# A looped adjacency kernel written out straight, with block 0 loaded in whole chunks from two queues

## The chip, the cores and the metric

The kernel runs on one core of one Trainium2 chip. The metric is device time in microseconds (us), from three runs of the kernel before: 1064.25, 1066.31 and 1069.69, with a median of 1066.31.

## The reference

`x` is 8192x256, `adj` is 8192x8192 and `w` (L0_gnn_weight) is 256x256, all float32.

```
bw  = sign(w)                       # -1, 0, 1
ba  = maximum(sign(x), 0)           # 1 where x > 0
xw  = ba @ bw.T                     # 8192 x 256
agg = relu(adj @ xw)                # 8192 x 256, the large product
y   = x + agg
out = (y - mean(y)) / sqrt(var(y) + 1e-5)   # over each row of 256
```

`adj` alone is 268 MB, and it is read once.

## The kernel before

**Blocks, chunks, units.** The 8192 output rows are cut into 16 blocks of 512. A block needs all 8192 columns of its rows of `adj`, in 8 chunks of 1024 columns (2 MB each). A chunk lands in one of four slots of `raw` as four DMAs, one for each group of 32 partitions (a quadrant); in it each contiguous run is 256 elements, 1024 bytes. A chunk is 4 units, so a block is 32 units and the kernel 512.

**A unit.** `turn` (DVE, L450) transposes 32x32 squares into `turned` in SBUF, or for 10 of 32 units into `turned_v` in PSUM. `make_hi` (ACT, L326) rounds it to fp32r into one of six buffers of a ring. The rest, `lo`, is made by POOL (L299) for the 22 "P" units and by DVE (L456) for the 10 "V" units. `use_unit` (PE, L619) multiplies both parts with `xw`: 8 matmuls of 512 columns, or 8 pairs of weight load and matmul. The accumulators of a block are two banks of PSUM, and blocks alternate between two sets.

**The steps of xw.** `xw` (64 slices of 128x256) is made in 16 groups of four slices: `make_step` (DVE, L414) compares `x` with zero, `turn_step` (PE, L576) transposes it, a copy brings it to SBUF, `make_xw` (PE, L587) multiplies it with the signs of `w`, and `copy_xw` (ACT, L316) stores it over the `x` that it came from. Groups 0 to 9 are made ahead of the units (their middle copy is DVE's, L422, `copy_early_step`), in PSUM banks that they alternate between; groups 10 to 15 stand between units 0 to 24 (middle copy by ACT, L312, `copy_late_step`). Two units use one group.

**Loads of block 0.** All of block 0 is loaded from SP's queue: `x` in 32 DMAs of 256 KB (L205), in runs of 1024 bytes, and `adj` in 16 parts of two units (64 DMAs of 256 KB, L217), in runs of 512 bytes. ACT's queue takes part from block 1 on: SP starts the quadrants 0 and 1 of a chunk, ACT the quadrants 2 and 3 (`start_chunk`, L195), SP as soon as DVE has turned the last unit of the chunk four before, ACT in its own order after `make_hi` of that unit.

**The ending of a block** runs between the units of the next one: `make_relu` on ACT (L336) at its unit 5, `turn_back` on PE (L644, 8 transposes) after its unit 4, the sum with the rows of `x` and the statistics on DVE (L460 to L475), and `normalise` on ACT (L344). `make_relu` at unit 5 of ACT's order comes ahead of PE's unit 4, as ACT runs ahead.

**Loops.** Each engine's program is a function `pair(q)` of two blocks. Pair 0 is written out, and pairs 1 to 7 are a hardware loop, `Fori(1, PAIRS)`, on SP, POOL, DVE and PE. On ACT the loop has pairs 1 to 6, `Fori(1, PAIRS - 1)`, and pair 7 is written out behind it. In the loops the semaphore values and the source address of `adj` come from the loop's register. In time, the back edges of ACT's loop fall at the ends of blocks 3, 5, 7, 9 and 11; at the end of block 13 ACT leaves its loop, and the other engines take their last back edge.

```
            pair(0)
            with act.Fori(1, PAIRS - 1) as q:
                pair(q)
            pair(PAIRS - 1)
```

Of the kernel before, what the change touches and what calls it, by code (L numbers as in the profile page):

```python
# [3 lines left out]

P = 128
Q = 32
G = P // Q  # L20
BANK = 512


def build(nc, x, adj, w, out):
# [8 lines left out]
    PAIRS = NBLK // 2  # L33
# [5 lines left out]
    KB = KG // Q  # L39
    UK = 2  # L40
# [3 lines left out]
    UP = 2 * UB  # L44
# [4 lines left out]
    UPP = 2  # L49
    PARTS = UB // UPP  # L50
    XPARTS = 8
    XK = CH * KB // XPARTS
# [3 lines left out]
    EARLY = 10  # L56
    TURNED = UPP
    STEP_BUFS = 2

    def late(g, delay):  # L60


        return 3 * (g - EARLY) + delay

    STEP, TURN, COPY, XW, XW_COPY = 2, 2, 5, 4, 9
    assert all(late(g, XW_COPY) < g * UPG for g in range(EARLY, GROUPS))


# [3 lines left out]

    kinds = ["V" if n % UB * V_UNITS % UB < V_UNITS else "P" for n in range(UP)]
    per_pair = {k: kinds.count(k) for k in "PV"}

    assert per_pair["P"] % TP == 0 and "VV" not in "".join(kinds + kinds[:1])

    def known_met(value):

        return isinstance(value, int) and value <= 0  # L80

    def in_pair(n):

        return kinds[:n].count(kinds[n])

    def ordinal(q, n):

        return q * per_pair[kinds[n]] + in_pair(n)

    def ring_slot(n):  # L90

        s = n % RING
        return s, n - RING if n >= RING else max(m for m in range(UP) if m % RING == s) - UP


    adj_v = adj.rearrange("(q h t i) (c g k) -> q h c g i t k", h=2, t=NT, i=Q, c=CH, g=G)
    x_turn = x.rearrange("(c g b j) d -> c g j b d", c=CH, g=G, b=KB)
    x_rows = x.rearrange("(q h m p) d -> q h p m d", h=2, m=MT, p=P)
    out_rows = out.rearrange("(q h m p) d -> q h p m d", h=2, m=MT, p=P)
# [3 lines left out]
    with ctx:  # L103
# [37 lines left out]

        ps_xw = [ps[:, 2 * b * BANK:2 * (b + 1) * BANK].rearrange("p (k d) -> p k d", k=GK) for b in range(2)]
        xw_buf = [g % 2 if g < EARLY else 1 for g in range(GROUPS)]
# [4 lines left out]

        w_loaded = sem("w_loaded")
        x_loaded = [sem(f"x_loaded{i}") for i in range(XPARTS)]  # L150
        parts_loaded = [sem(f"parts_loaded{i}") for i in range(PARTS)]
# [11 lines left out]
        early_steps_copied = sem("early_steps_copied")  # L163
        late_steps_copied = sem("late_steps_copied")
# [21 lines left out]

        LOWER, UPPER = range(0, G // 2), range(G // 2, G)
        IN_TURNS = [g for both in zip(LOWER, UPPER) for g in both]  # L190

        def start_chunk(eng, q, h, c, quadrants):
            dst = raw[:, c % SLOTS, :].rearrange("p (t k) -> p t k", t=NT)
            for g in quadrants:
                eng.dma_start(dst[g * Q:(g + 1) * Q], adj_v[q, h, c, g]).then_inc(adj_loaded[c % SLOTS], 16)  # L195

        @block.sync
        def _(sp):
            sp.dma_start(w_sb, w_rows).then_inc(w_loaded, 16)

            def load_x(i):

                c, k = i * XK // KB, i * XK % KB
                for g in IN_TURNS:
                    sp.dma_start(x_sb[g * Q:(g + 1) * Q, i * XK:(i + 1) * XK],  # L205
                                 x_turn[c, g, :, k:k + XK]).then_inc(x_loaded[i], 16)

            def load_part(i):

                c, u = i * UPP // UPC, i * UPP % UPC  # L210
                k0, k1 = u * UK * Q, (u + UPP) * UK * Q
                dst = raw[:, c % SLOTS, :].rearrange("p (t k) -> p t k", t=NT)
                if c >= SLOTS:

                    sp.wait_ge(units_turned, (c - SLOTS) * UPC + u + UPP)
                for g in IN_TURNS:
                    sp.dma_start(dst[g * Q:(g + 1) * Q, :, k0:k1],  # L217
                                 adj_v[0, 0, c, g, :, :, k0:k1]).then_inc(parts_loaded[i], 16)

            def load_chunk(q, h, c):  # L220
                n = (q * 2 + h) * CH + c

                sp.wait_ge(units_turned, (n - SLOTS + 1) * UPC)
                start_chunk(sp, q, h, c, LOWER)

            def block_before(q, h):
                return (q, 0) if h else (q - 1, 1)

            def store_rows(q, h):
                sp.wait_ge(blocks_done, q * 2 + h + 1)  # L230
                sp.dma_start(out_rows[q, h], rows[:]).then_inc(rows_stored, 16)

            def load_rows(q, h):
                b = q * 2 + h
                if known_met(b):
# [5 lines left out]
                sp.dma_start(rows[:], x_rows[q, h]).then_inc(rows_loaded, 16)  # L241

            def load_block_0():

                early = EARLY * GK // XK
                for i in range(early - 1):
                    load_x(i)
                for i in range(PARTS):
                    for j in range(early, XPARTS):
                        if late(j * XK // GK, STEP) == i * UPP:  # L250
                            load_x(j)
                    load_part(i)
                    if i == 0:
                        load_x(early - 1)

            def load_block(q, h):
                for c in range(CH):
                    load_chunk(q, h, c)

                    if c == 2 and not known_met(q * 2 + h - 1):  # L260
                        store_rows(*block_before(*block_before(q, h)))
                    if c == 3:
                        load_rows(*block_before(q, h))

            load_block_0()
            load_block(0, 1)
            with sp.Fori(1, PAIRS) as q:
                for h in range(2):
                    load_block(q, h)
            store_rows(PAIRS - 1, 0)  # L270
            load_rows(PAIRS - 1, 1)
            for b, ms in PIECES:
                if b == NBLK - 1:
                    sp.wait_ge(blocks_done, NBLK)
                else:
                    sp.wait_ge(last_piece_done, 1)
                sp.dma_start(out_rows[PAIRS - 1, 1, :, ms[0]:ms[-1] + 1],
                             rows[:, ms[0]:ms[-1] + 1]).then_inc(rows_stored, 16)
            sp.wait_ge(rows_stored, (NBLK - 1 + len(PIECES)) * 16)

        @block.gpsimd
        def _(pool):
# [8 lines left out]
            def pair(q):  # L291
                for n in range(UP):
                    if kinds[n] != "P":
                        continue
                    t = in_pair(n) % TP
                    s, _ = ring_slot(n)

                    pool.wait_ge(his_made, q * UP + n + 1)  # L298
                    pool.tensor_tensor(lo[:, s], turned[:, t], hi[:, s].bitcast(f32),  # L299
                                       ALU.subtract).then_inc(p_los_made, 1)  # L300

            pair(0)
            with pool.Fori(1, PAIRS) as q:
                pair(q)

        @block.scalar
        def _(act):
            def copy_late_step(n):
                act.wait_ge(steps_turned, n + 1)

                act.wait_ge(xw_made, n - 1)
                act.activation(step_xT[:, n % 2], ps_xT[n % 2], ACT.Copy).then_inc(late_steps_copied, 1)  # L312

            def copy_xw(n):
                act.wait_ge(xw_made, n + 1)
                act.activation(xw[:, n * GK:(n + 1) * GK], ps_xw[xw_buf[n]], ACT.Copy).then_inc(xw_copied, 1)  # L316

            def make_hi(q, n):
                s, prev = ring_slot(n)
                act.wait_ge(units_turned, q * UP + n + 1)  # L320
                if not known_met(q * UP + prev + 1):

                    act.wait_ge(units_used, q * UP + prev + 1)
                t = in_pair(n)
                src = turned[:, t % TP] if kinds[n] == "P" else turned_v
                act.activation(hi[:, s], src, ACT.Copy).then_inc(his_made, 1)  # L326

            def make_relu(q, h):
                b = q * 2 + h
                act.wait_ge(first_halves, b + 1)  # L330
                if not known_met(b):
                    act.wait_ge(relus_turned, b * MT)
                for a in range(DH):
                    if a == 1:
                        act.wait_ge(units_used, (b + 1) * UB)
                    act.activation(relu[:, a], acc[h][a], ACT.Relu).then_inc(relus_made, 1)  # L336

            def make_std(b, ms):
                act.wait_ge(mvs_made, b + 1)
                act.activation(std[:, ms], mv[:, ms, 1], ACT.Sqrt, bias=eps[:]).then_inc(stds_made, 1)  # L340

            def normalise(b, m, last):
                act.wait_ge(shifts_made, b + 1)
# [5 lines left out]
            def ending(q, h, u):  # L349

                if u == RING - 1:
                    make_relu(q, h)
# [341 lines left out]
```

## Time and profile before

| | us |
|---|---|
| Median of the runs (1064.25 to 1069.69) | 1066.31 |
| Span of the profiled execution, first to last instruction | 1064.2 |
| PE busy with matmuls | 993.5 |
| DVE busy | 858.2 |
| POOL busy | 840.3 |
| ACT busy | 605.2 |
| Data moved | 294.36 MB, 277 GB/s over the span |
| Mean granted TensorE clock | 0.976 |

The span is one profiled execution and not one of the three runs; the device time of that execution is not given by itself, so the span is the profiled execution's own time here. An average over the span hides the stages: block 0, the blocks after it, and the last few microseconds each have another limit.

### The profile page before, as it was taken

To read this page: it belongs to the slowest core of one execution; us is meant where nothing else is said; L and a number is where in the kernel's file an instruction comes from. 1 tells how busy PE (TensorE), PEld (TensorE's weight loads), DVE (VectorE), ACT (ScalarE), POOL (GpSimd) and SP (SyncE) were. 2 spreads that over 40 slices of the span, in tenths; PEclk is the share of its full clock that TensorE was granted. 3 is DMA by queue.
4 is the path that set the end of the run, shared out by engine and by line. 5 is a ranking of instruction groups with operands and counts; after the bars stand their busy time and mean duration, and the time that the engine had idled before them with its cause. 6 is when DMAs were issued, how large, how long until landed. Compare 5 with 4: busy or idle time off the path is not lost.

```text
span 1064.2 us, 15065 instructions
## 1 busy us (share of the span) xinstructions
PE 993.5 (93%) x4484; PEld 812.8 (76%) x4484; DVE 858.2 (81%) x881; ACT 605.2 (57%) x647; POOL 840.3 (79%) x361
## 2 busy tenths in 40 slices
PE   5578699999998999899998999899998999999996
PEld 4356578888877888788886888778886888888885
DVE  4656489898959989598886989599895989799893
ACT  3345366666546656466565665466564665566562
POOL 0346489899868988599896998599885998889893
PEclk9889899999999999999999999989999999999999
DMA  9999999999998999899998999999998999999961
GB/s 216 226 223 224 228 286 320 302 332 317 308 315 241 292 324 282 250 295 311 299 297 250 300 313 294 290 236 289 327 284 253 300 306 299 300 290 297 309 198 39
DMA packets 313166, 294.36 MB, mean 277 GB/s; under 512 B 9760, under 2 KB 313120, under 8 KB 313120
## 3 DMA queue, kind: packets, MB, share of 16 engines
q1 hardware_dynamic: 186400, 168.06, 62.3%
q10 hardware_dynamic: 126720, 125.84, 42.3%
q14 instruction: 36, 0.29, 0.1%
q8 instruction: 10, 0.16, 0.1%
HBM read 285.47 MB, written 8.39 MB: 276 GB/s over the span
## 4 chain that ended last, share of the span: by engine, by line
PE 44%; POOL 26%; issue 12%; SPq 9%; DMA 4%; DVE 3%; ACT 1%; POOLq 0%; ACTq 0%
PE ps L619 44%; POOL lo L299 26%; SPq L217 7%; DMA raw<-in_adj_dram 4%; SPq L205 2%; DVE turned L450 1%; DVE lo L456 1%; PE ps L644 1%; DVE ps L450 0%; ACT hi L326 0%; DVE relu L414 0%; DVE stats L464 0%; POOLq L298 0%; SPq L195 0%; ACT rows L344 0%
## 5 line engine op out<-in xcount | busy, mean ns | idle before, releaser
L299 POOL TENSOR_TENSOR lo<-turned,hi 128x1024 fp32r<-128x1024 f32 x352 | 839.2, 2413 | 207.1 <-ACT hi L326 203.9
L619 PE MATMUL ps<-hi,xw 128*128 128x512 f32 x2048 | 810.0, 396 | 31.8 <-DVE lo L456 27.1
L619 PE MATMUL ps<-lo,xw 128*128 128x512 f32 x2048 | 804.8, 393 | 0.0
L326 ACT ACTIVATE hi<-turned 128x1024 fp32r<-128x1024 f32 x352 | 373.4, 1061 | 281.4 <-DVE turned L450 161.7
L619 PEld LDWEIGHTS ps<-hi,xw 128*128 128x128 f32 x2048 | 389.6, 190 | 120.0 <-DVE lo L456 24.9
L619 PEld LDWEIGHTS ps<-lo,xw 128*128 128x128 f32 x2048 | 389.4, 190 | 80.4
L450 DVE STREAM_TRANSPOSE turned<-raw 128x1024 f32<-128x1024 f32 x352 | 426.1, 1218 | 22.3 <-DMA raw<-in_adj_dram 22.3
L456 DVE TENSOR_TENSOR lo<-ps,hi 128x1024 fp32r<-128x1024 f32 x160 | 194.8, 1217 | 128.1 <-ACT hi L326 127.5
L326 ACT ACTIVATE hi<-ps 128x1024 fp32r<-128x1024 f32 x160 | 164.1, 1025 | 134.4 <-issue 58.9
L450 DVE STREAM_TRANSPOSE ps<-raw 128x1024 f32<-128x1024 f32 x160 | 195.1, 1219 | 18.6 <-DMA raw<-in_adj_dram 18.6
L344 ACT ACTIVATE rows<-rows,shift,rstd 128x256 f32<-128x256 f32 x62 | 36.4, 588 | 0.0
L587 PE MATMUL ps<-sign_wT,rows 128*128 128x256 bf16 x128 | 21.3, 325 | 13.1 <-ACT xw L316 11.5
L460 DVE TENSOR_TENSOR rows<-ps,rows 128x1024 f32<-128x1024 f32 (+1 forms) x17 | 19.4, 1139 | 13.5 <-PE ps L644 12.2
L587 PEld LDWEIGHTS ps<-sign_wT,rows 128*128 128x128 bf16 x128 | 13.7, 115 | 19.2 <-issue 13.3
L414 DVE TENSOR_SCALAR relu<-x_sb 128x1024 bf16<-128x1024 f32 x16 | 16.6, 1046 | 12.4 <-DMA x_sb<-in_x_dram 12.4
L316 ACT ACTIVATE xw<-ps 128x1024 fp32r<-128x1024 f32 x16 | 16.3, 1020 | 12.5 <-PE ps L587 12.5
L576 PE MATMUL ps<-ident_b,relu 128*128 128x128 bf16 x128 | 12.0, 254 | 11.9 <-DVE relu L414 11.9
L336 ACT ACTIVATE relu<-ps 128x512 f32<-128x512 f32 x32 | 17.2, 586 | 9.2 <-PE ps L619 9.2
L464 DVE BATCH_NORM_STATS2 stats<-rows 128x6 f32<-128x256 f32 x64 | 22.3, 409 | 0.1
L576 PEld LDWEIGHTS ps<-ident_b,relu 128*128 128x128 bf16 x128 | 9.7, 116 | 15.0 <-DVE relu L414 13.2
L644 PE MATMUL ps<-ident,relu 128*128 128x128 f32 x128 | 16.8, 273 | 0.2 <-ACT relu L336 0.2
L644 PEld LDWEIGHTS ps<-ident,relu 128*128 128x128 f32 x128 | 14.8, 140 | 2.7 <-ACT relu L336 0.4
(23 smaller groups left out, 47.8 us busy)
## 6 DMA issues: line engine op xcount, KB each, us to landing
raw<-in_adj_dram ACTq DMA_DIRECT2D x240, 512.0 KB, 10.4
raw<-in_adj_dram SPq DMA_DIRECT2D x240, 512.0 KB, 9.0
raw<-in_adj_dram SPq DMA_DIRECT2D x64, 256.0 KB, 7.4
x_sb<-in_x_dram SPq DMA_DIRECT2D x32, 256.0 KB, 8.1
rows<-in_x_dram SPq DMA_DIRECT2D x16, 512.0 KB, 8.8
out_dram<-rows SPq DMA_DIRECT2D x15, 512.0 KB, 13.7
out_dram<-rows SPq DMA_DIRECT2D x2, 256.0 KB, 2.3
rows<-in_L_gnn_weight_dram SPq DMA_DIRECT2D x1, 256.0 KB, 3.7
```

The lines of the kernel that those rows point to most:

```text
L205: sp.dma_start(x_sb[g * Q:(g + 1) * Q, i * XK:(i + 1) * XK], x_turn[c, g, :, k:k + XK]).then_inc(x_loaded[i], 16)
L217: sp.dma_start(dst[g * Q:(g + 1) * Q, :, k0:k1], adj_v[0, 0, c, g, :, :, k0:k1]).then_inc(parts_loaded[i], 16)
L299: pool.tensor_tensor(lo[:, s], turned[:, t], hi[:, s].bitcast(f32), ALU.subtract).then_inc(p_los_made, 1)
L326: act.activation(hi[:, s], src, ACT.Copy).then_inc(his_made, 1)
L344: done = act.activation(rows[:, m], rows[:, m], ACT.Identity, bias=shift[:, m:m + 1], scale=rstd[:, m:m + 1])
L450: dve.transpose(dst.rearrange("p (k t j) -> p k t j", k=UK, j=Q), src).then_inc(units_turned, 1)
L456: dve.tensor_tensor(lo[:, s], turned_v[:, :], hi[:, s].bitcast(f32), ALU.subtract).then_inc(v_los_made, 1)
L464: dve.bn_stats(stats[:, m], rows[:, m]).then_inc(stats_made, 1)
L576: last = pe.transpose(ps_xT[n % 2][:, k, i], step_x[:, n % STEP_BUFS, k, i * P:(i + 1) * P], ident_b[:])
L587: last = pe.matmul(ps_xw[xw_buf[n]][:, k], step_xT[:, n % 2, k, i], sign_wT[:, i], start=(i == 0), stop=(i == DH - 1))
L619: return pe.matmul(acc[h][a], xw[:, step, a * P:(a + 1) * P], part[:, s, k * MB:(k + 1) * MB], start=(step == 0 and part is hi), stop=(ste ...
L644: last = pe.transpose(back[:, m, a * P:(a + 1) * P], relu[:, a, m * P:(m + 1) * P], ident[:])
```

## The change

The program becomes straight on every engine: no loops, and all semaphore values and addresses are constants. The order of the units, the engine that takes each, the ring and the endings are the same. In block 0:

- `adj` comes from both queues, SP the quadrants 0 and 1, ACT the quadrants 2 and 3. Chunk 0 comes in two halves (runs of 512 bytes, 8 DMAs of 256 KB), chunks 1 to 7 whole (runs of 1024 bytes, 28 DMAs of 512 KB).
- `x` comes from both queues too, in 9 pieces (36 DMAs): two of four slices for chunk 0, then one of eight slices for each chunk, issued just ahead of the chunk.
- ACT issues `x` and chunks 0 and 1 ahead of its first copy, `x` and chunk 2 ahead of `copy_xw(0)`, `x` and chunk 3 after `make_hi(1)`, and from then on a chunk (with its `x` in block 0) after each fourth unit.
- Only groups 0 and 1 of the steps start ahead of the units; the others stand between the units of block 0, one group for each two units. ACT makes all the middle copies, and one pair of PSUM banks holds the product.

```diff
+    X_PIECES = [(0, GK), (GK, GK)] + [(c * KB, KB) for c in range(1, CH)]
...
         @block.sync
+            for i in range(2):
+                start_x(sp, i, LOWER)
+                start_half(sp, i, LOWER)
...
+            for c in range(1, CH):
+                start_x(sp, c + 1, LOWER)
+                load_chunk(c)
+            for b in range(1, NBLK):
                 for c in range(CH):
-                    load_chunk(q, h, c)
+                    load_chunk(b * CH + c)
...
         @block.scalar
-            act.wait_ge(idents_made, 3)
-            for g in range(EARLY - XK // GK):
-                copy_xw(g)
-            for n in range(TURNED):
-                make_hi(0, n)
-            for g in range(EARLY - XK // GK, EARLY):
-                copy_xw(g)
-            pair(0)
-            with act.Fori(1, PAIRS - 1) as q:
-                pair(q)
-
-            pair(PAIRS - 1)
...
+            for i in range(2):
+                start_x(act, i, UPPER)
+                start_half(act, i, UPPER)
+            start_x(act, 2, UPPER)
+            start_chunk(act, 1, UPPER)
+            copy_step(0)
+            start_x(act, 3, UPPER)
+            start_chunk(act, 2, UPPER)
+            copy_xw(0)
+            for n in range(UNITS):
+                make_hi(n)
+                if n == 0:
+                    copy_step(1)
+                if n == 1:
+                    start_x(act, 4, UPPER)
+                    start_chunk(act, 3, UPPER)
+                ch = n // UPC + SLOTS
+                if n % UPC == UPC - 1 and ch < NCHUNK:
+                    if ch < CH:
+                        start_x(act, ch + 1, UPPER)
+                    start_chunk(act, ch, UPPER)
+                if n < UB:
+                    g = n // UPG + 1
+                    if n % UPG and 2 <= g < GROUPS:
+                        copy_step(g)
+                    if n % UPG and g - 1 >= 1:
+                        copy_xw(g - 1)
+                else:
+                    ending(n // UB - 1, n % UB)
...
         @block.vector
-            dve.wait_ge(signs_turned, 1)
-            dve.tensor_copy(sign_wT[:], ps_wT).then_inc(signs_copied, 1)
...
             make_step(0)
-            for g in range(1, EARLY):
...
-            pair(0)
-            with dve.Fori(1, PAIRS) as q:
-                pair(q)
+            dve.wait_ge(signs_turned, 1)
+            dve.tensor_copy(sign_wT[:], ps_wT).then_inc(signs_copied, 1)
+            for n in range(UNITS):
+                turn(n)
+                if n == 0:
+                    make_step(1)
+                if n and kinds[n - 1] == "V":
+                    make_lo(n - 1)
+                c = n // UPC + 1
+                if n % UPC == UPC - 1 and c < CH:
+                    for g in range(c * KB // GK, (c + 1) * KB // GK):
+                        make_step(g)
+                if n >= UB:
+                    ending(n // UB - 1, n % UB)
...
         @block.tensor
-            pair(0)
-            with pe.Fori(1, PAIRS) as q:
-                pair(q)
-            turn_back(PAIRS - 1, 1)
+            turn_step(0)
+            pe.wait_ge(signs_copied, 1)
+            make_xw(0)
+            turn_step(1)
+            for n in range(UNITS):
+                use_unit(n)
+                if n < UB and n % UPG == 0:
+                    g = n // UPG
+                    if g + 1 < GROUPS:
+                        make_xw(g + 1)
+                    if g + 2 < GROUPS:
+                        turn_step(g + 2)
+                if n >= UB and n % UB == BACK_AT:
+                    turn_back(n // UB - 1)
+            turn_back(NBLK - 1)
```

`UNITS` is 512, `UB` 32 (units of a block), `UPC` 4 (of a chunk), `UPG` 2 (of a group), `SLOTS` 4. `make_xw(n)` waits for `copy_step(n)` and `copy_xw(n - 1)`, `use_unit` of an even unit 2g of block 0 for `copy_xw(g)`, and `copy_step(n)` for `make_xw(n - 2)`.

## Rows read from the trace of the kernel before

**Rows 1.** The page: busy time of each engine, and GB/s in 40 slices.
```profile
PE 993.5 (93%) x4484; PEld 812.8 (76%) x4484; DVE 858.2 (81%) x881; ACT 605.2 (57%) x647; POOL 840.3 (79%) x361
...
GB/s 216 226 223 224 228 286 320 302 332 317 308 315 241 292 324 282 250 295 311 299 297 250 300 313 294 290 236 289 327 284 253 300 306 299 300 290 297 309 198 39
```

**Rows 2.** Timeline of PE, the transposes of the block endings (start us, us, engine, line).
```profile
150.42 1.04 PE L644 MATMUL ps<-ident,relu 128*128 128x128 f32 x8
...
209.37 1.03 PE L644 MATMUL ps<-ident,relu 128*128 128x128 f32 x8
...
268.29 1.04 PE L644 MATMUL ps<-ident,relu 128*128 128x128 f32 x8
...
333.27 1.03 PE L644 MATMUL ps<-ident,relu 128*128 128x128 f32 x8
...
828.03 1.03 PE L644 MATMUL ps<-ident,relu 128*128 128x128 f32 x8
...
1004.83 1.04 PE L644 MATMUL ps<-ident,relu 128*128 128x128 f32 x8
```

**Rows 3.** Timeline, ACT and PE behind the end of block 3.
```profile
320.00 1.02 ACT L326 ACTIVATE hi<-ps 128x1024 fp32r<-128x1024 f32 x1 [11.39 <-issue]
...
322.34 0.50 PE L619 MATMUL ps<-hi,xw 128*128 128x512 f32 x1 [4.01 <-DVE lo L456]
```

**Rows 4.** Timeline of ACT behind the end of block 13, where it leaves its loop.
```profile
937.09 1.07 ACT L326 ACTIVATE hi<-turned 128x1024 fp32r<-128x1024 f32 x1 [0.75 <-PE ps L619]
937.11 0.87 ACTq L195 DMA_DIRECT2D raw<-in_adj_dram  x2
938.08 1.03 ACT L326 ACTIVATE hi<-ps 128x1024 fp32r<-128x1024 f32 x1
```

**Rows 5.** Windows: busy us (x instructions) by engine, PEclk, DMA share, GB/s.
```profile
0.00:4.00 4.00, 0.00 (x0) 0.00 (x0) 0.00 (x0) 0.00 (x0) 1.12 (x9) 1.00 0.54 128
...
4.00:16.00 12.00, 6.07 (x41) 4.52 (x42) 6.04 (x10) 2.31 (x2) 0.00 (x0) 1.00 1.12 236
60.00:90.00 30.00, 20.36 (x111) 15.79 (x111) 21.70 (x18) 16.18 (x17) 14.39 (x7) 0.89 1.21 224
...
172.00:192.00 20.00, 20.00 (x90) 16.57 (x89) 18.89 (x18) 14.35 (x17) 19.53 (x10) 1.00 1.10 347
936.00:948.00 12.00, 12.00 (x59) 10.02 (x58) 11.33 (x11) 9.19 (x11) 12.00 (x6) 1.00 1.12 235
```

**Rows 6.** The page, queue of ACT: packets, MB, share.
```profile
q10 hardware_dynamic: 126720, 125.84, 42.3%
```

**Rows 7.** Timeline: DMAs issued by SP and ACT in block 0 (start, duration of issue).
```profile
1.23 11.16 SPq L205 DMA_DIRECT2D x_sb<-in_x_dram  x16
...
26.51 18.86 SPq L217 DMA_DIRECT2D raw<-in_adj_dram  x12
...
92.00 4.81 ACTq L195 DMA_DIRECT2D raw<-in_adj_dram  x1
...
97.45 1.03 ACT L326 ACTIVATE hi<-ps 128x1024 fp32r<-128x1024 f32 x1 [3.67 <-issue]
```

**Rows 8.** Timeline of PE in block 0: a product of xw, a unit, transposes, a unit.
```profile
85.42 1.03 PE L587 MATMUL ps<-sign_wT,rows 128*128 128x256 bf16 x8 [3.09 <-ACT xw L316]
86.21 0.47 PE L619 MATMUL ps<-hi,xw 128*128 128x512 f32 x1
...
88.14 0.62 PE L576 MATMUL ps<-ident_b,relu 128*128 128x128 bf16 x8
88.57 0.47 PE L619 MATMUL ps<-hi,xw 128*128 128x512 f32 x1
...
90.50 0.40 PE L619 MATMUL ps<-hi,xw 128*128 128x512 f32 x1
```

**Rows 9.** Timeline of ACT in block 0.
```profile
98.37 1.02 ACT L312 ACTIVATE rows<-ps 128x1024 bf16<-128x1024 bf16 x1
99.28 1.06 ACT L326 ACTIVATE hi<-turned 128x1024 fp32r<-128x1024 f32 x1
100.22 1.02 ACT L316 ACTIVATE xw<-ps 128x1024 fp32r<-128x1024 f32 x1
```

**Rows 10.** The page, costliest groups: busy, mean ns, idle before.
```profile
L299 POOL TENSOR_TENSOR lo<-turned,hi 128x1024 fp32r<-128x1024 f32 x352 | 839.2, 2413 | 207.1 <-ACT hi L326 203.9
...
L450 DVE STREAM_TRANSPOSE turned<-raw 128x1024 f32<-128x1024 f32 x352 | 426.1, 1218 | 22.3 <-DMA raw<-in_adj_dram 22.3
```

More of the change, by code:

```diff
@@ L55, in build, with ordinal, piece_of_group @@
     UPG = GK // UK
-    EARLY = 10
-    TURNED = UPP
     STEP_BUFS = 2
[L60 to L66, printed above, removed]
+    BACK_AT = 4
     PIECES = [(NBLK - 1, range(0, MT // 2)), (NBLK, range(MT // 2, MT))]
[L73 to L96, printed above, removed]
+    kinds = ["V" if n * V_UNITS % UB < V_UNITS else "P" for n in range(UB)] * NBLK
+    before = {k: [0] * (UNITS + 1) for k in "PV"}
+    for n, kind in enumerate(kinds):
+        for k in "PV":
+            before[k][n + 1] = before[k][n] + (k == kind)
+    assert "VV" not in "".join(kinds) and kinds[-1] == "P"
+    def ordinal(n):
+        return before[kinds[n]][n]
+    X_PIECES = [(0, GK), (GK, GK)] + [(c * KB, KB) for c in range(1, CH)]
+    def piece_of_group(g):
+        return g if g < KB // GK else g * GK // KB + 1
+    adj_v = adj.rearrange("(b t i) (c g k) -> b c g i t k", t=NT, i=Q, c=CH, g=G)
     x_turn = x.rearrange("(c g b j) d -> c g j b d", c=CH, g=G, b=KB)
-    x_rows = x.rearrange("(q h m p) d -> q h p m d", h=2, m=MT, p=P)
-    out_rows = out.rearrange("(q h m p) d -> q h p m d", h=2, m=MT, p=P)
+    x_rows = x.rearrange("(b m p) d -> b p m d", m=MT, p=P)
+    out_rows = out.rearrange("(b m p) d -> b p m d", m=MT, p=P)
     w_rows = w.rearrange("(a p) i -> p a i", p=P)
@@ L139, in build @@
         turned_v = ps[:, 4 * BANK:6 * BANK]
-        ps_xw = [ps[:, 2 * b * BANK:2 * (b + 1) * BANK].rearrange("p (k d) -> p k d", k=GK) for b in range(2)]
-        xw_buf = [g % 2 if g < EARLY else 1 for g in range(GROUPS)]
+        ps_xw = ps[:, 2 * BANK:4 * BANK].rearrange("p (k d) -> p k d", k=GK)
         ps_xT = [ps[:, b * BANK:(b + 1) * BANK].bitcast(bf16).rearrange("p (k a n) -> p k a n", k=GK, a=DH)
@@ L199, in _, with load_chunk, store_rows, load_rows @@
             sp.dma_start(w_sb, w_rows).then_inc(w_loaded, 16)
[L201 to L235, printed above, removed]
+            for i in range(2):
+                start_x(sp, i, LOWER)
+                start_half(sp, i, LOWER)
+            def load_chunk(ch):
+                if ch >= SLOTS:
+                    sp.wait_ge(units_turned, (ch - SLOTS + 1) * UPC)
+                start_chunk(sp, ch, LOWER)
+            def store_rows(b):
+                sp.wait_ge(blocks_done, b + 1)
+                sp.dma_start(out_rows[b], rows[:]).then_inc(rows_stored, 16)
+            def load_rows(b):
+                if b == 0:
                     sp.wait_ge(xw_made, GROUPS)
@@ L240, in load_rows @@
                     sp.wait_ge(rows_stored, b * 16)
[L241 to L256, printed above, removed]
+                sp.dma_start(rows[:], x_rows[b]).then_inc(rows_loaded, 16)
+            for c in range(1, CH):
+                start_x(sp, c + 1, LOWER)
+                load_chunk(c)
+            for b in range(1, NBLK):
                 for c in range(CH):
-                    load_chunk(q, h, c)
-                    if c == 2 and not known_met(q * 2 + h - 1):
-                        store_rows(*block_before(*block_before(q, h)))
+                    load_chunk(b * CH + c)
+                    if c == 2 and b >= 2:
+                        store_rows(b - 2)
                     if c == 3:
[L263 to L271, printed above, removed]
+                        load_rows(b - 1)
+            store_rows(NBLK - 2)
+            load_rows(NBLK - 1)
             for b, ms in PIECES:
@@ L289, in _ @@
                                    pattern=[[-1, P]], channel_multiplier=1).then_inc(idents_made, 1)
[L291 to L299, printed above, removed]
+            for n in range(UNITS):
+                if kinds[n] == "P":
+                    pool.wait_ge(his_made, n + 1)
+                    pool.tensor_tensor(lo[:, n % RING], turned[:, ordinal(n) % TP], hi[:, n % RING].bitcast(f32),
@@ L314, in copy_xw @@
             def copy_xw(n):
                 act.wait_ge(xw_made, n + 1)
[L316 to L326, printed above, removed]
@@ L328, in make_relu, with make_hi @@
-            def make_relu(q, h):
-                b = q * 2 + h
+                act.activation(xw[:, n * GK:(n + 1) * GK], ps_xw, ACT.Copy).then_inc(xw_copied, 1)
+            def make_hi(n):
+                act.wait_ge(units_turned, n + 1)
+                if n >= RING:
+                    act.wait_ge(units_used, n - RING + 1)
+                src = turned[:, ordinal(n) % TP] if kinds[n] == "P" else turned_v
+                act.activation(hi[:, n % RING], src, ACT.Copy).then_inc(his_made, 1)
@@ L330, in make_relu @@
+            def make_relu(b):
                 act.wait_ge(first_halves, b + 1)
-                if not known_met(b):
+                if b:
                     act.wait_ge(relus_turned, b * MT)
@@ L366, in pair @@
-            def pair(q):
-                for n in range(UP):
-                    if not (known_met(q) and n < TURNED):
-                        make_hi(q, n)
-                        load_chunk_after(q, n)
-                    for g in range(EARLY, GROUPS):
-                        if known_met(q) and n == late(g, COPY):
-                            copy_late_step(g)
-                        if known_met(q) and n == late(g, XW_COPY):
-                            copy_xw(g)
-                    if n < UB and not known_met(q):
-                        ending(q - 1, 1, n)
-                    if n >= UB:
-                        ending(q, 0, n - UB)
@@ L397, in _ @@
+            make_relu(NBLK - 1)
+            for n, ms in PIECES:
+                make_std(n, slice(ms[0], ms[-1] + 1))
+            n, ms = PIECES[0]
             for m in ms:
-                normalise(b, m, m == ms[-1])
+                normalise(n, m, m == ms[-1])
         @block.vector
@@ L580, in make_xw @@
             def make_xw(n):
-                wait_step_copied(n)
-                if n >= 2:
-                    pe.wait_ge(xw_copied, max(m for m in range(n) if xw_buf[m] == xw_buf[n]) + 1)
+                pe.wait_ge(steps_copied, n + 1)
+                if n >= 1:
+                    pe.wait_ge(xw_copied, n)
                 for k in range(GK):
                     for i in range(DH):
-                        last = pe.matmul(ps_xw[xw_buf[n]][:, k], step_xT[:, n % 2, k, i], sign_wT[:, i],
+                        last = pe.matmul(ps_xw[:, k], step_xT[:, n % 2, k, i], sign_wT[:, i],
@@ L647, in turn_back @@
                             last.then_inc(relus_turned, 1)
-            BACK_AT = 4
-            def pair(q):
-                for n in range(UP):
-                    for g in range(EARLY, GROUPS):
-                        if known_met(q) and n == late(g, TURN):
-                            turn_step(g)
-                        if known_met(q) and n == late(g, XW):
-                            make_xw(g)
-                    use_unit(q, n)
-                    if n == BACK_AT and not known_met(q):
-                        turn_back(q - 1, 1)
-                    if n == UB + BACK_AT:
-                        turn_back(q, 0)
-            pair(0)
-            with pe.Fori(1, PAIRS) as q:
-                pair(q)
-            turn_back(PAIRS - 1, 1)
+            turn_step(0)
+            pe.wait_ge(signs_copied, 1)
+            make_xw(0)
+            turn_step(1)
+            for n in range(UNITS):
+                use_unit(n)
[8 more added lines that the diff above has]
+            turn_back(NBLK - 1)
 _INS = ['x', 'adj', 'L0_gnn_weight']
```

221 lines of the change are left out of this document (84 added, 137 removed).

## The prediction

> **What bounds the kernel now.** I read the page first, then the stages. PE is busy 93% of the span and the others less; the slices of GB/s [rows 1] fall into a start of some 140 us at about 225 GB/s and a rest near 300, with a dip at 241, 250, 250, 236 and so on every 120 us or so. So there are three stages: block 0, the blocks after it, and their interruptions.
>
> The transposes of the endings stand at one place of every block and serve as a clock [rows 2]. Where nothing interferes two of them are 58.95 or 58.92 us apart, and the last three blocks take (1004.83 - 828.03) / 3 = 58.93 each. That is PE itself: 256 matmuls at 0.227 plus 0.87 for the transposes. POOL needs 22 x 2.41 = 53.1 of them, DVE has 32 turns at 1.22 and 10 los [rows 10]. From 150.42 to 1004.83 are 14 blocks, 14 x 58.93 = 825.0, but 854.4 passed: 29.4 us are lost. They are lost behind blocks 3, 5, 7, 9 and 11, and nowhere else (268.29 to 333.27 is 64.98, 6.05 too much; the other four cost 5.5 to 6.5). There ACT stands 11.39 us with no releaser, only "issue", and PE waits 4.01 for the lo behind it [rows 3], then runs its first matmuls at the lower clock. Those are the five places where ACT's loop takes its back edge. Behind block 13 all the other engines take theirs, ACT does not, and ACT goes on without a gap [rows 4]. So ACT's back edge costs, and theirs does not.
>
> The span is thus: ending of block 0 at T1 = 150.42, 825.0 for 14 blocks, 29.4 lost, and 59.4 from the last ending's place to the end (1064.2 - 1004.83).
>
> In block 0 PE is busy about two thirds of the time (20.4 of 30 us) while the DMA share is full [rows 5]: data bound it. One queue moves 236 GB/s in runs of 1024 bytes (the first x) and 224 with runs mostly of 512, so the length of the runs alone is worth 5%. With both queues filled it is 347 [rows 5]. Behind block 13 it falls to 235 again, in runs of 1024 bytes, for 12 us.
>
> **The change, part by part.**
>
> *Straight program.* No back edge remains: minus 29.4 us. What must hold is that straight code of this length is fetched in time; ACT's pairs 0 and 7 are straight now, and pair 7 shows no gap at its start [rows 4]. In the loops the waits on register values vanish too, which I cost at nothing: PE's 58.93 hides them. The 14 blocks now follow one another without a rest for the DMA queues. A block needs 16.8 MB of adj and 1 MB of rows in 58.93 us, 302 GB/s, against 347 when both queues are full [rows 5]; so 825.0 stays.
>
> *Bytes of block 0.* x is 8.39 MB, adj 16.78, w 0.26: 25.4 MB. At 347 GB/s, with 1.8 us of start (4 us at 128 GB/s are 2.2 us at 236 [rows 5]), the last chunk would have landed at 75; halves of chunk 0 are 512-byte runs, and I put everything up to them at 300. Between 236 and 347 this landing is at 110 to 75. Before, T1 less five units puts the end of block 0 at 141.
>
> *PE in block 0.* Two units share a group of xw. From the rows: product 0.79 (85.42 to 86.21), a unit 1.93 (86.21 to 88.14), transposes 0.43, a unit 1.93 [rows 8]: 5.08 us for two units, 81 us for the block. PE's order makes a chain: even unit 1.93, product 0.79, transposes 0.62 until their end, then on ACT the middle copy and copy_xw, 0.92 and 1.02 [rows 9], and only then the next even unit: 5.4 with 0.1 for the handing over. So 5.4 per group, 10.8 per chunk; a chunk and its x are 3.15 MB, 9.1 us at 347. Fully loaded, PE's chain is slower than the data. ACT has 2 x 1.05 + 1.94 = 4.0 in those 5.4, POOL at most 4.8: hidden.
>
> *ACT's own DMA issues.* This is the part that costs. A queue takes only so much: by 12.39 us SP had issued 16 x DMAs, 4,096 runs [rows 7], while 0.51 MB + 8.4 us x 236 GB/s - 0.26 = 2.2 MB had moved: 1,900 runs were outstanding, and SP needed 0.70 us for each issue. By 45.37 it had issued 14,336 runs and some 12,700 had moved, 1,650 outstanding. I take 1,750 to 1,800 runs as the limit (packets of ACT's queue are one for a run of 1024 bytes, [rows 6]). Now ACT issues the same amounts, and its copies stand behind. Its half of x and chunks 0 and 1 is 4,096 runs, x and chunk 2 and each later one 1,536 more. So copy_step(0) has to wait until 2,300 runs of ACT's have moved, copy_xw(0) for 3,830, make_hi(2) for 5,370, and copy_step(2), behind unit 3 and chunk 4, for 6,900. Those are for both halves 3.1, 6.0, 9.2 and 12.3 MB, or 12, 21, 30 and 39 us (3.4 MB at 300, the rest at 347). PE starts unit 0 at about 23, and unit 2 waits for copy_xw(1), which ACT does behind copy_step(2): 40.7. Chunk 5 is behind unit 7, at 47.5, where its room is there at 47.8: from then on ACT no longer waits. Nothing of this is seen on ACT now but one issue of 4.81 us, behind which a hi stood 3.67 us late [rows 7].
>
> From unit 2 on: 15 groups, 14 x 5.4 + 3.9 = 79.5, plus 2 for the lower clock after PE's idle 13 us, gives 122 for the end of block 0. Five units of block 1, 9.3, give T1 = 131.5 against 150.4: minus 18.9.
>
> **Sum.** 131.5 + 825.0 + 59.4 = 1015.9 against the profiled 1064.2, so minus 48.3. The median of the runs is 2.1 above that span: 1066.3 - 48.3 = 1018.0.
>
> **A rule that speaks against it.** The Trainium skill, in "DMA: Bandwidth & Descriptors", section "Issuing engines are not separate DMA queues", says that DMAs started by several engines run on the same 16 DMA engines and that the only saving is the issuing time. The trace disagrees for this shape: 235 to 236 with one queue, 347 with two [rows 5]. By the rule block 0 would stay at 236; that is rival 2.
>
> **Rivals.**
>
> 1. *ACT's issues don't hold it.* For: in the steady blocks two DMAs of ACT take 0.87 [rows 4]. Against: there its queue is never full, and SP's was [rows 7]. Then unit 4 starts as chunk 1 has landed (22.5) and been turned, at 27.5; 14 groups later, less 1.5 for the last, it is 101.6, T1 = 111, and the time 997.
>
> 2. *The two queues don't add up in block 0*, where x and adj are mixed: 236 GB/s. A chunk with x takes 13.4 us, ACT waits for 12.3 MB until 54, and again ahead of chunk 8: 8,704 + 3 x 1,536 + 1,024 - 1,800 runs, 107 us, with 12 units left after unit 19: 32 us more. T1 = 148, and only the 29.4 and 2 are won: 1035.
>
> 3. *The gaps stay.* ACT's 11.39 has no releaser in the profile; that the back edge makes it is read from where it falls. If it comes back as often in straight code, 29.4 stay: 1047.
>
> 4. *Slower: straight code stalls.* A fetch that costs ACT 11 us and PE 5.9 would come at each stretch of code not seen before, and now all of it is new. The mechanism needs more than 48.3 / 5.9 = 8 such gaps beyond the five of now to lose: two in each of 14 blocks, 28 in all, are 23 more than now, plus 136 - 18.9: 1183; one for each block, 14, gives 1066 + 53 - 18.9 = 1100. Against it: no such gap in the straight pairs.
>
> Beside rivals 3 and 4 stands a rule: the Trainium skill, in "Runtime: NRT & Kernel Launch", section "Instruction fetch mechanics", has straight code fetched ahead and a taken branch outside the fetched pages wait for its target. By it both rivals fall; the trace agrees at ACT's five back edges and shows no cost at the other engines'.
>
> **How the numbers follow.** Forecast: 0.50. Its own range is 1008 to 1028: with 355 GB/s and a limit of 2,050 runs copy_step(2) comes 2 us earlier, with 310 and 1,500 it comes 5 later, and 15 groups at 5.1 to 5.6 are 4.5 less or 3 more. Rival 1: 0.18. Rival 2: 0.14. Rival 3: 0.07. Rival 4: 0.06. Nothing gained, for a reason that I don't see: 0.05. The range takes in rivals 1 and 2 and ends just beyond them, 995 to 1036; rivals 3 and 4 and the last case are left out, 0.18. A measurement of this kernel tells about 0.5% from no change, 5.3 us. Faster by more: forecast, rivals 1, 2 and 3, and a little of the last, 0.90. Same 0.03, slower 0.07.
>
> **What would show it.** Right: transposes of the endings 58.93 apart from first to last, no idle "issue" on ACT behind block 1; first of them near 131; ACT's DMA issues of several us each before unit 4, and "issue" as what ended ACT's idle time there; PE idle for over 10 us ahead of unit 2; 330 GB/s or more from 15 to 60 us. Wrong: issues of 0.4 us on ACT and a first ending at 111 (rival 1); a rate of 236 in block 0 (rival 2); ACT idle for 11 us at regular places (rivals 3 and 4), or waits for raw in the blocks after 0, which would tell that the DMA needed its rests.

## The result, and the profile after

The changed kernel takes 1021.75 us (median; 1067.2 before, in four runs each): 0.958 of the time before, with a 95% interval of 0.955 to 0.960. The forecast was 1018.0. One of the four executions took 1054.4 and is left out of the ratio; it has no trace, and e4's profiled one, 1055.6, shows what such an execution can look like. The profiled execution has a span of 1019.9 and a device time of 1021.75.

| | before | after |
|---|---|---|
| Span of the profiled execution | 1064.2 | 1019.9 |
| First ending's transposes (T1) | 150.4 | 134.9 |
| From there to the last ending but one (14 blocks) | 854.4 | 825.1 |
| From there to the end | 59.4 | 59.9 |

Timeline of PE in the kernel after, the transposes of the endings (start us, us, engine, line). They answer to [rows 2].

```profile
134.87 1.04 PE L500 MATMUL ps<-ident,relu 128*128 128x128 f32 x8
...
193.82 1.03 PE L500 MATMUL ps<-ident,relu 128*128 128x128 f32 x8
...
959.98 1.04 PE L500 MATMUL ps<-ident,relu 128*128 128x128 f32 x8
```

Two endings are 58.95 us apart, and (959.98 - 134.87) / 14 is 58.94: no block loses anything now. 29.3 us of the gain are there, and 15.5 in block 0. The page's rows for [rows 1]:

```profile
PE 977.7 (96%) x4484; PEld 802.9 (79%) x4484; DVE 846.3 (83%) x871; ACT 614.0 (60%) x657; POOL 841.7 (83%) x361
...
GB/s 284 346 314 230 180 294 310 307 283 315 297 305 306 317 297 291 327 286 302 299 318 292 299 294 315 297 304 323 274 317 291 317 291 311 321 277 320 288 180 41
```

The dips to 240 and 250 every 120 us are gone, and the start has 346 where it had 225. The fourth and fifth slices, 230 and 180, are low for another reason: by then the data are ahead of PE, and SP waits until DVE has turned the units of a chunk and freed its slot. The windows of block 0 (busy us by engine, PEclk, DMA share, GB/s), for [rows 5]:

```profile
4.00:16.00 12.00, 3.65 (x24) 2.65 (x25) 5.25 (x7) 2.31 (x2) 0.00 (x0) 1.00 1.17 283
16.00:40.00 24.00, 8.23 (x40) 5.87 (x37) 7.72 (x7) 7.85 (x9) 7.02 (x3) 0.89 1.10 346
...
60.00:90.00 30.00, 27.50 (x164) 20.45 (x162) 21.29 (x20) 19.55 (x21) 16.63 (x8) 1.00 1.08 280
```

PE is busy for 8.2 of the 24 us from 16 to 40, while the queues move data at 346 GB/s. What it waits for stands in ACT's timeline (bracket: idle before, and what ended it):

```profile
4.87 3.40 ACTq L169 DMA_DIRECT2D x_sb<-in_x_dram  x2
8.30 3.17 ACTq L155 DMA_DIRECT2D raw<-in_adj_dram  x2
...
12.80 1.02 ACT L240 ACTIVATE rows<-ps 128x1024 bf16<-128x1024 bf16 x1
...
15.22 4.49 ACTq L155 DMA_DIRECT2D raw<-in_adj_dram  x2
19.75 1.02 ACT L244 ACTIVATE xw<-ps 128x1024 fp32r<-128x1024 f32 x1 [5.93 <-issue]
...
24.73 4.41 ACTq L155 DMA_DIRECT2D raw<-in_adj_dram  x2
29.19 1.06 ACT L251 ACTIVATE hi<-turned 128x1024 fp32r<-128x1024 f32 x1 [5.64 <-DVE ps L352]
...
33.43 4.42 ACTq L155 DMA_DIRECT2D raw<-in_adj_dram  x2
37.95 1.02 ACT L240 ACTIVATE rows<-ps 128x1024 bf16<-128x1024 bf16 x1 [6.76 <-issue]
```

Issues of 0.3 to 0.5 us elsewhere take 2.2 each here. The 5.64 us ahead of `make_hi(2)` are put down to DVE, but the copy starts at 29.19, just as the issue of 24.73 ends (29.14): there too the issue ended last. ACT's first copy starts at 12.8, copy_xw(0) at 19.75, make_hi(2) at 29.19 and copy_step(2) at 37.95 (forecast: 12, 21, 30, 39). PE's unit 2 follows:

```profile
39.95 0.79 PE L475 MATMUL ps<-hi,xw 128*128 128x512 f32 x1 [9.36 <-ACT xw L244]
```

### The profile page after: what moved, and what is told of

Its sections match the earlier page's. It is cut to its first block, busy times and chain, and to the rows that moved or that the text cites. A ratio compares the mean times of both kernels' runs of the same rounds, so it can differ in the third digit from the quotient of the medians.

```text
span 1019.9 us, 12240 instructions
## 1 busy us (share of the span) xinstructions
PE 977.7 (96%) x4484; PEld 802.9 (79%) x4484; DVE 846.3 (83%) x871; ACT 614.0 (60%) x657; POOL 841.7 (83%) x361
## 4 chain that ended last, share of the span: by engine, by line
PE 92%; ACTq 3%; ACT 2%; issue 2%; DVE 1%; DVEq 0%
PE ps L475 89%; ACTq L155 2%; PE ps L500 1%; ACT xw L244 1%; ACTq L169 1%; PE ps L460 1%; PE ps L450 1%; DVE relu L330 1%; ACT hi L251 0%; ACTq L162 0%; DVE stats L364 0%; ACT L240 0%; DVE rows L360 0%; ACT rows L240 0%; ACT relu L260 0%
## 5 line engine op out<-in xcount | busy, mean ns | idle before, releaser
L475 PEld LDWEIGHTS ps<-hi,xw 128*128 128x128 f32 x2048 | 385.6, 188 | 102.7 <-ACT xw L244 17.1
L240 ACT ACTIVATE rows<-ps 128x1024 bf16<-128x1024 bf16 x16 | 16.4, 1025 | 34.8 <-PE ps L450 28.0
L460 PE MATMUL ps<-sign_wT,rows 128*128 128x256 bf16 x128 | 18.8, 295 | 6.1 <-ACT rows L240 6.1
L500 PEld LDWEIGHTS ps<-ident,relu 128*128 128x128 f32 x128 | 14.8, 140 | 2.7 <-ACT relu L260 0.4
## 6 DMA issues: line engine op xcount, KB each, us to landing
rows<-in_x_dram SPq DMA_DIRECT2D x16, 512.0 KB, 11.3
```

The costliest lines, as they stand in the source:

```text
L460: last = pe.matmul(ps_xw[:, k], step_xT[:, n % 2, k, i], sign_wT[:, i], start=(i == 0), stop=(i == DH - 1))
L475: return pe.matmul(acc[b % 2][a], xw[:, step, a * P:(a + 1) * P], part[:, n % RING, k * MB:(k + 1) * MB], start=(step == 0 and part is hi) ...
L500: last = pe.transpose(back[:, m, a * P:(a + 1) * P], relu[:, a, m * P:(m + 1) * P], ident[:])
```

## The experiments

Those on the kernel before are e1 and e2; all others are edits of the changed kernel. Each was timed against the kernel before, whose medians were 1064.97 to 1067.41 in these sessions.

**e1: ACT's loop alone written out.**

```diff
-            with act.Fori(1, PAIRS - 1) as q:
+            for q in range(1, PAIRS - 1):
                 pair(q)
```

> The kernel before with ACT's loop alone written out; block 0 and the loops of SP, POOL, DVE and PE stay. Theory (only ACT's back edge costs, 5.9 us of PE each): the five gaps go, 29.4 us less, about 1037.5, and the endings' transposes stand 58.93 apart from block 1 on. Rival (the gap comes with the amount of ACT's code, not with the back edge): ACT still stands 11 us at five or more places, 1067 or more. Rival (the other engines' back edges cost PE too and hide behind ACT's): between 1040 and 1067.

Measured: 1035.94, a ratio of 0.972 (0.968 to 0.975). The endings' transposes in its timeline:

```profile
149.25 1.03 PE L644 MATMUL ps<-ident,relu 128*128 128x128 f32 x8
...
974.36 1.03 PE L644 MATMUL ps<-ident,relu 128*128 128x128 f32 x8
```

14 blocks take 825.1, or 58.94 each, with the loops of the four other engines in place. So ACT's loop alone, with its back edges, made the 29.4. The time is 1.6 below the 1037.5 expected.

**e2: the loops of SP, POOL, DVE and PE written out, ACT's left.** The edit is that of e1 on the other four engines.

> The kernel before with the loops of SP, POOL, DVE and PE written out, ACT's loop left. Theory: no change, 1067, ACT's five gaps of 11 us and PE's of 4 us remain behind blocks 3, 5, 7, 9 and 11. Rival (others' back edges cost as well): 5 us or more faster. Rival (long straight code of PE costs fetches): slower, by 5.9 us for each.

Measured: 1067.62 (median of ten) beside 1065.77 before, which is 1.002 of it. The ratio of 0.996 (0.990 to 1.001) takes in only the three lowest of the ten. Either way there is no change. ACT's gap stands where it stood:

```profile
320.03 1.02 ACT L326 ACTIVATE hi<-ps 128x1024 fp32r<-128x1024 f32 x1 [11.33 <-issue]
```

One of the ten executions took 1050.5; it has no trace, and why is open. Together e1 and e2 settle rivals 3 and 4 of the prediction: straight code has no gaps of its own, neither on ACT nor on PE.

**e3: all loads of block 0 on SP's queue, in the changed kernel's pieces.**

```diff
-                start_x(sp, i, LOWER)
-                start_half(sp, i, LOWER)
+                start_x(sp, i, IN_TURNS)
+                start_half(sp, i, IN_TURNS)
...
-                start_x(sp, c + 1, LOWER)
+                start_x(sp, c + 1, IN_TURNS)
```

`IN_TURNS` are the quadrants 0, 2, 1, 3, so that the one queue changes between the halves of the partitions. `load_chunk` does the same for block 0, and ACT starts none of its DMAs there.

> The changed kernel with all loads of block 0 on SP's queue, in the same pieces (runs of 1024 bytes but for chunk 0), and none on ACT. Theory (the rate comes from the two queues, the length of the runs gives 5%): 236 GB/s in block 0, the last chunk lands near 110 us, ACT's issues no longer hold it, first ending near 132, time about 1019. Rival (the rate of 347 comes from whole chunks in long runs, whichever queue): 347 GB/s from SP alone, no stalls of ACT, first ending near 111, time about 998.

Measured: 1036.23, ratio 0.972 (0.969 to 0.976): 14.5 slower than the changed kernel. Its windows, and the first ending:

```profile
4.00:16.00 12.00, 4.52 (x28) 2.91 (x28) 6.10 (x8) 4.24 (x5) 0.00 (x0) 1.00 1.15 235
16.00:40.00 24.00, 16.87 (x71) 12.69 (x72) 14.01 (x11) 10.62 (x11) 11.65 (x5) 0.88 1.13 225
...
60.00:90.00 30.00, 23.97 (x132) 17.46 (x131) 17.18 (x15) 16.03 (x18) 15.09 (x6) 0.94 1.13 225
```

```profile
149.48 1.03 PE L488 MATMUL ps<-ident,relu 128*128 128x128 f32 x8
```

The rate is 225 with runs of 1024 bytes, as the 224 with runs of mostly 512 before [rows 5]. So whole chunks bring nothing by themselves: the first ending is at 149.5, where it was before, and block 0's gain needs ACT's queue beside SP's.

The expected 132 for that ending was 17 too early. 25.4 MB at 225 instead of 236 is 5 later. The rest stands in DVE's timeline, at the first unit of chunk 7:

```profile
126.76 1.25 DVE L340 STREAM_TRANSPOSE turned<-raw 128x1024 f32<-128x1024 f32 x1 [3.76 <-DMA raw<-in_adj_dram]
```

By then 28.5 MB had moved (counted by queue in the trace), 2.6 of them on ACT's queue and all for block 1: they went ahead of chunk 7, which needs only block 0's 25.4.

The same trace says two things more. The first is that a second queue alone does not bring the rate. From 96 to 112 us both queues move data, SP 1.9 MB (all quadrants) and ACT 1.8 MB (quadrants 2 and 3), and the sum is that of one queue. In the kernel before it is the same from 98 to 118, 228 GB/s.

```profile
96.00:112.00 16.00, 10.41 (x63) 7.66 (x62) 1.37 (x2) 5.47 (x6) 2.37 (x1) 0.91 1.12 235
```

346 came only where SP's queue writes the quadrants 0 and 1 and ACT's the quadrants 2 and 3. Whether the separate halves make it is not tested: no run has two queues over the same halves throughout. The DMA share does not tell the two cases apart, 1.12 at 235 and 1.10 at 346.

The second is that an issue can be slow with nothing ahead of it on its own queue. This is the first DMA that ACT starts in e3, while SP's queue is full; its first bytes move at 93.4.

```profile
80.98 7.00 ACTq L156 DMA_DIRECT2D raw<-in_adj_dram  x1
```

**e4: ACT issues the same DMAs later among its copies.**

```diff
+            later = {1: 2, 3: 3, 5: 4, 7: 5, 11: 6, 15: 7}
...
+                    if n in later:
+                        start_x(act, later[n] + 1, UPPER)
+                        start_chunk(act, later[n], UPPER)
```

Chunk 1 goes behind `copy_step(0)`, and the old places of the issues are gone.

> The changed kernel; ACT issues the same DMAs of block 0 later among its copies: chunk 1 behind the first middle copy, chunk 2 behind unit 1, chunks 3, 4 and 5 behind the copies of units 3, 5 and 7. Theory (units 0 to 3 wait because ACT stands in issues of chunks that they don't need): unit 2 starts near 26 us instead of 39.9, first ending near 122 instead of 134.9, time about 1009. Rival (block 0 is bound by its data or by PE's chain, whatever ACT does early): less than 2 us gained, 1020 to 1022. Rival (ACT's queue runs empty and the rate falls to 236 at times): first ending above 135, slower than 1022.

Measured: 1015.99, ratio 0.954 (0.950 to 0.957), 5.8 less where 13 were expected. Of its five executions the profiled one took 1055.6, late chunks from 480 us on; block 0 is read from it, where it is not disturbed. The first ending is at 128.74. In ACT's timeline units 2 and 3 come at 19.75 instead of 29.19 and 30.16, behind a first stall of 3.3, but three longer ones follow, ahead of units 4, 6 and 8:

```profile
29.19 1.02 ACT L251 ACTIVATE hi<-ps 128x1024 fp32r<-128x1024 f32 x1 [5.61 <-issue]
...
37.99 1.06 ACT L251 ACTIVATE hi<-turned 128x1024 fp32r<-128x1024 f32 x1 [5.01 <-issue]
...
48.23 2.00 ACT L251 ACTIVATE hi<-turned 128x1024 fp32r<-128x1024 f32 x2 [6.44 <-issue]
```

A chunk behind each two units is more than the queue drains: the stall moves with the issue. That ACT's issues bind is shown; how much is to be had was not, so far.

**e5: copy_xw ahead of the next middle copy.**

```diff
+                    if n % UPG and g - 1 >= 1:
+                        copy_xw(g - 1)
                     if n % UPG and 2 <= g < GROUPS:
                         copy_step(g)
-                    if n % UPG and g - 1 >= 1:
-                        copy_xw(g - 1)
```

> The changed kernel; in block 0 ACT makes copy_xw ahead of the middle copy of the next group. Theory (the chain unit, product, transposes, two copies sets 5.48 us for two units): a copy leaves the chain and PE's own 5.08 is left, 0.4 us x 13 groups = 5 us less, about 1016.5. Rival (PE's own work or the waits on lo set the period): no change.

Measured: 1014.95, ratio 0.951 (0.950 to 0.953), first ending at 128.98: 5.9 less. The median is 6.8 less, where 5 were expected. The chain through ACT's two copies was real.

**e6: DVE makes the steps ahead of the lo.** In the kernel after, ACT's middle copies follow one another by 5.47 to 5.51 us but for two places of 7.5, at unit 11 (56.67 to 64.16) and unit 27. DVE's timeline there:

```profile
59.56 1.23 DVE L356 TENSOR_TENSOR lo<-ps,hi 128x1024 fp32r<-128x1024 f32 x1 [5.41 <-ACT hi L251]
60.70 3.35 DVE L330 TENSOR_SCALAR relu<-x_sb 128x1024 bf16<-128x1024 f32 x2
```

and PE's:

```profile
63.51 0.62 PE L450 MATMUL ps<-ident_b,relu 128*128 128x128 bf16 x8 [1.84 <-DVE relu L330]
```

Units 10 and 26 are V units and next to last in their chunk, so DVE waits with their lo for ACT and only then makes the steps that PE's transposes need. The edit moves the loop over `make_step` ahead of `make_lo`.

> The changed kernel; DVE makes the two steps at the end of a chunk ahead of the lo of the unit before. Theory (at units 11 and 27 that lo waits for ACT's hi, and PE's transposes wait for the step behind it, 2 us each): the two periods of 7.5 us become 5.5, 4 us less, about 1017.7. Rival (the steps are late for their x or for the step buffers): no change.

Measured: 1018.28, ratio 0.954 (0.953 to 0.956), first ending at 130.52, 4.35 earlier. Its profiled execution, 1022.5, lost 5 us again, in the blocks after 0, to late chunks, most of them between 480 and 760.

**e7: e4, e5 and e6 together.**

> The changed kernel with ACT's issues later, copy_xw first and the steps ahead of the lo, all three. Theory: they add up, 13 + 5 + 4 = 22 us less, near 1000, limited by the landing of the chunks: chunk 7 lands at 77 and PE needs 10.2 us for a chunk, so the data does not bind. Rival (with PE faster the data of block 0 binds): the gain stops at about 15 us, 1007.

Measured: 1009.46, ratio 0.947 (0.944 to 0.950), first ending at 120.07, in six executions from 1007.1 to 1016.9. 14.8 in block 0, close to what the three gave singly (6.1 + 5.9 + 4.35 = 16.4). The 22 expected are missed because e4's part was put at 13. The time is near the rival's 1007, but e10 below shows that the data of block 0 were not the limit here. Every group of two units in the middle of block 0 now takes PE's own time (transposes behind products, 5.06 apart):

```profile
59.98 0.61 PE L445 MATMUL ps<-ident_b,relu 128*128 128x128 bf16 x8
...
65.03 0.61 PE L445 MATMUL ps<-ident_b,relu 128*128 128x128 bf16 x8
...
70.09 0.61 PE L445 MATMUL ps<-ident_b,relu 128*128 128x128 bf16 x8
```

**e8: ACT's issues of block 0 spread out.**

```diff
-            later = {1: 2, 3: 3, 5: 4, 7: 5, 11: 6, 15: 7}
+            later = {1: 2, 5: 3, 9: 4, 12: 5, 15: 6, 18: 7}
```

> As e7, with ACT's issues of chunks 3 to 7 of block 0 spread to stand behind units 5, 9, 12, 15 and 18 (in e7: 3, 5, 7, 11 and 15, where ACT still stood in four issues, 21 us in all, up to 48 us). Theory (the queue takes some 2,000 runs, 1.3 chunks with x; a chunk for each four units never fills it): no gaps of ACT after 20 us, unit 2 near 24, 15 groups at 5.06, first ending near 109 instead of 120.1, time near 997. Rival (the queue runs empty or the chunks land late): waits for raw in block 0, first ending at 115 or more. The blocks after 0 may still lose some us to late chunks, as in e7.

Measured: 1007.54, ratio 0.945 (0.943 to 0.946), in seven executions from 1006.8 to 1026.3; first ending at 121.19. The expected 109 was missed, and block 0 is no shorter than in e7 (120.07). From 20 to 47 us no copy of ACT waited for an issue, but chunks 5 to 8 stand close together, and there ACT had four waits of 2.3, 2.5, 4.6 and 4.7, each of which ended as an issue ended (seen in e9's trace, which has the same schedule; the last of them):

```profile
69.24 5.70 ACTq L155 DMA_DIRECT2D raw<-in_adj_dram  x2
74.99 1.02 ACT L241 ACTIVATE xw<-ps 128x1024 fp32r<-128x1024 f32 x1 [4.71 <-issue]
```

**e9: e8, with the rows stored from ACT's queue.** In SP's program the stores of blocks 0 to 14 go, and ACT has:

```diff
+                if u == 27:
+                    act.wait_ge(blocks_done, b + 1)
+                    act.dma_start(out_rows[b], rows[:]).then_inc(rows_stored, 16)
```

> As e8, with the store of each block's rows issued by ACT at unit 27 in place of SP in the next block. Now SP's queue moves 9.4 MB a block and ACT's 8.4; this makes it 8.9 and 8.9. Theory (in straight blocks of 58.93 us SP's queue is the one that falls behind, 302 GB/s wanted of 347): the late chunks of e7's blocks 13 and 14 go, the runs lie closer together (within 3 us) and the median is 2 to 5 us below e8. Rival (the lag is of the memory, not of a queue): scatter and median as e8.

Measured: 1006.38, ratio 0.943 (0.942 to 0.945), five executions from 1005.9 to 1007.7. The longest waits of e8 from 120 us on have these two rows:

```profile
DVE turned L348 <- DMA raw<-in_adj_dram: 18.8, 11, 4.1
...
DVE rows L356 <- DMA rows<-in_x_dram: 15.6, 8, 2.3
```

e9's have no wait for a DMA at all. The medians are 1.2 apart, less than expected; the scatter went from 19 us to 2. Three of e8's seven executions lie above 1009, none of e9's five. The edit moves the store to another queue and also to another time, and it is not separated which of them counts.

**e10: e9, with ACT's chunks 3 to 10 behind units 5, 9, 13, 17, 21, 24, 27 and 30.**

> As e9, with ACT's chunks 3 to 10 issued behind units 5, 9, 13, 17, 21, 24, 27 and 30. In e8 and e9 ACT had no stall up to 47 us, but chunks 5 to 8 stood close together (units 12, 15, 18, 19) and ACT stood in them up to 75 us, which cost PE 8 us and the lower clock. Theory: without that clump PE keeps its 5.06 for two units, first ending near 111 instead of 121.4, time near 996. Rival (some other wait holds block 0 at 120): no change, 1006.

Measured: 996.72, ratio 0.935 (0.934 to 0.937), five executions from 996.0 to 997.8. The first ending:

```profile
109.69 1.03 PE L496 MATMUL ps<-ident,relu 128*128 128x128 f32 x8
```

That is 11.7 earlier than e9's 121.37. It is the fastest kernel of this study, 25 us ahead of the change. Its data begin to bind: from 20 to 110 us DVE waits 14.4 us for `raw`.

**e11: the changed kernel with e9's edit alone.**

> The changed kernel with nothing changed but the store of each block's rows, issued by ACT at unit 27 in place of SP. Theory (SP's queue carries 9.4 of 17.8 MB a block and falls behind in some executions): median as the changed kernel or up to 1 us less, 1020.5 to 1022, and all runs within 3 us of each other. Rival (the late chunks don't depend on the queues' balance): runs of 1025 to 1055 are among them, as with the changed kernel.

Measured: 1021.45, ratio 0.958 (0.956 to 0.960). Five executions lie from 1020.8 to 1022.0; a sixth took 2566, which is left out; it has no trace, and why is open. The median is the changed kernel's, as expected; the few executions don't exclude the rival here, and e8 against e9 is the better test.

## Why the prediction was right

**The gaps.** Minus 29.4 forecast, minus 29.3 measured, and e1 and e2 show the cause. Beside it, the Trainium skill has a taken branch whose target lies outside the fetched pages wait for its code ("Runtime: NRT & Kernel Launch", "Instruction fetch mechanics"). ACT's idle 11.3 us at its back edge agree with that; e2 shows the back edges of four other engines at no cost to the time. That the 11.3 us are a fetch is not shown by any run.

**825.0 for 14 blocks.** 825.1. Where all goes well 302 GB/s are had without a rest. But the step that called it safe, "against 347 when both queues are full", was too good. The rate of 347 needs both queues filled, and SP's carried 9.4 of 17.8 MB; that this split makes chunks late is argued, not shown. The profiled executions of e6, e7 and e8 lost 5 to 8 us behind block 0, and e4's lost 40, to late chunks, which the sum has not.

**The two queues.** 346 GB/s measured for 347 forecast, with 283 in the first 16 us for the 300 taken. Rival 2 is refuted by the 346. Of the Trainium skill's rule in "DMA: Bandwidth & Descriptors", "Issuing engines are not separate DMA queues", by which starting DMAs from several engines saves issuing time only, e3 shows both sides: with the same pieces 225 GB/s from one queue and 346 from two with a half of the partitions each, against the rule, but 235 from two queues while SP's carried all quadrants, with it. So "with both queues filled it is 347" leaves out a condition; the change happened to meet it. Rival 2's own sum is off too: at 236 GB/s the room for chunk 8 is there at 103 us, not 107, which makes T1 144 and the time 1031. The runs' length, to which I gave 5%, gives nothing on one queue (225 against 224).

**ACT's issues.** The four times came out within 1.3 us of the forecast, and unit 2 at 39.95 for 40.7; PE's idle time ahead of it was 9.4 us, not over 10. As the four groups of issues end, 2,140, 1,920, 1,790 and 1,800 runs of ACT's are outstanding (issued less moved, counted in the trace), for 1,750 to 1,800 taken. e4 and e10 show that the issues, not the data or PE, held block 0 there: e10 won another 11.7 over e9 by moving nothing else but issues. One reading does not fit: the issue of 4.81 us at 92.00 in the kernel before [rows 7] was ACT's first DMA of all, as was that of 7.00 us in e3. A limit of the queue's own cannot have held them, and what did is open. Rival 1 (ACT not held, 997) was wrong for this kernel. e10 comes to that time, 996.7, by another way: less waiting on ACT and a shorter chain.

**The chain in block 0.** 5.4 forecast, 5.48 measured. The step that missed is "ACT has 2 x 1.05 + 1.94 = 4.0 in those 5.4, POOL at most 4.8: hidden", which leaves DVE's order out: at two chunk ends DVE's order puts a lo that waits for ACT ahead of the steps that PE waits for, 2.0 us each (e6: 4.35 in all). With the period's 0.08 in 14 groups that is 5.1 us; 0.75 of it came back at unit 2, and T1 was 134.9 instead of 131.5. So about 1 us more came back, which is not accounted for. The span is 4.0 above the forecast's 1015.9: 3.4 at T1, 0.1 in the 14 blocks, 0.5 behind them. The device time lies 1.85 above the span, not 2.1, which makes 3.75.

## What to carry to other kernels

A compute engine that issues DMAs is held in its issues once some 1,800 to 2,100 runs are outstanding on its queue (the kernel after), so its issues belong behind the work that paces them, evenly, and never in a clump ahead of a copy that others wait for (e10 against e9, 11.7 us). An empty queue is no guarantee: e3's first issue on ACT took 7.00 us while the other queue was full. Look at what falls together in time in a loop's period before unrolling anything: here one engine's back edge cost 5.9 us of PE each, and those of four others nothing. When a kernel stops pausing, its queues stop resting too, and in e8 against e9 that showed as scatter and hardly in the median; that the uneven split between the queues is the reason is likely, not shown.

## What the runs showed that I had not expected

One queue moves 225 to 235 GB/s, in runs of 512 or of 1024 bytes. Two move 346 where each writes its own half of the partitions, but 235 where SP's writes all quadrants beside ACT's (e3, 96 to 112 us). With both queues on halves of their own, runs of 512 bytes may matter: 283 GB/s from 4 to 16 us, where over half the bytes are chunk 0's, against 346 behind it; no experiment separates that from the start. And the store of 0.5 MB in each block, moved from one queue to the other and to another time, took the spread of the executions from 19 us to 2 (e8 against e9), though the median moved by 1.2.
